# Relu-squared attention: score banks freed by the relu, gate units on one ring bank, the output factor a slot later, output projection behind the last gate unit

## The chip, the cores and the metric

One core of a Trainium2 chip runs the whole kernel in one launch. The metric is the device time of the execution in microseconds. The engines of the core work side by side, each on its own queue of instructions, and meet by semaphores: TensorE (PE, with its weight loads PEld) does matrix products and transposes into PSUM, VectorE (DVE) and ScalarE (ACT) read PSUM and SBUF, GpSimd (POOL) works on SBUF and issues the indirect DMAs, SyncE (SP) issues the plain DMAs.

## The reference, cut to what matters

Four blocks follow each other on 16 sequences of 256 tokens with 128 channels: a linear-recurrence attention, a mixture of 32 experts, a relu-squared attention, and a transformer block with 8 experts. The change touches the third alone:

```python
qg = split_heads(tokens @ Wqg, 16); kv = split_heads(tokens @ Wkv, 16)
queries, gates = qg[..., :16], qg[..., 16:]
keys, values = kv[..., :16], kv[..., 16:]
queries, keys, values = l2norm(queries), l2norm(keys), l2norm(values)
attn = square(relu(einsum('bhid,bhjd->bhij', queries, keys)))
aggr = einsum('bhij,bhjd->bhid', attn, values)
out = tanh(norm(aggr)) * aggr / norm(aggr) * tanh(silu(gates))
x = x + out.reshape(b, n, 1024) @ Wout
```

## The kernel before, in words

The kernel runs stage after stage, with all engines meeting between them. In the attention stage `pipeline` (line 76) carries the 16 sequences through five places, one place a step: `fetch` (gather the expert rows, combine them, normalise), `front` (project queries, keys, values and gates), `att` (scores, relu, square, aggregate), `tail` (norm of the aggregate, its factor, gating) and `end` (last gating, output projection, x3). A step thus works on up to five sequences. Fetch runs in steps 0 to 15, front in 1 to 16, att in 2 to 17, tail in 3 to 18, end in 4 to 19.

Each engine's queue is written out by hand in its own `half`, as eight slots g = 0 to 7, one for each pair of heads. The order in the source is the order on the engine; nothing is planned or reordered. An engine that waits for a semaphore holds everything behind it.

Scores of pair g go to two of the four score banks of PSUM (`scores`, line 1147), by turns. ScalarE's `relu` (line 858) reads both banks and writes a tile of SBUF, one of a ring of four. Five of the eight tiles are squared on VectorE (`square`, line 1679), which before the change multiplies the score banks by the relu's result; two on ScalarE (line 865), one on POOL (line 613). So before the change TensorE may overwrite score banks only when both relu and VectorE's square are done. `aggregate` (line 1163) multiplies the squares with the values; `take_aggregate` (line 883) copies two pairs' worth and frees those banks.

All other products of TensorE share two ring banks, 0 and 1. `fill` (line 1139) waits for the readers of the bank's last content. The tables `G_BANK`, `FT_BANK` and `F_BANK` (line 344) say which bank a gate unit (`project_gate`), a turned factor (`turn_factor`) and a spread factor (`spread_factor`) take. A gate unit goes through `unit_tanh` on ScalarE and `silu_unit` on VectorE (line 1702), which frees its bank.

The tail's chain is: `sum_squares` on TensorE, `norm_of` on VectorE (line 1688), `length_of` on POOL (o_inv, line 632), `tanh_of_norm` on ScalarE, `split_factor` on POOL (lines 639 to 649), `turn_factor`, `take_factor` on ScalarE (line 901), `spread_factor`, `gate_unit` on VectorE (line 1696), `output_of` on POOL (line 656).

The front's query and key chain ends on VectorE: `v_sum` (line 1747), `inverse_root` (from line 1661), the scaling of queries and keys (line 1800), the copy of the high part on ScalarE (line 940), `split_terms` (lines 1754 to 1758). Then TensorE's `turn_terms` (line 1223) transposes the terms. POOL scales the values (line 680) behind `length_of(tail, 1)`. VectorE's `combine` (line 1715) mixes the gathered rows: eight instructions of line 1722 with three inputs, then statistics. x3 is formed on line 1807.

## Time and profile before

| | us |
|---|---|
| median of 3 runs | 1832.07 |
| the three runs | 1829.85, 1848.20, 1832.07 |
| the profiled execution | 1849.76 |
| its span | 1848.1 |
| TensorE busy | 1281.9 (69%) |
| VectorE busy | 1097.8 (59%) |
| POOL busy | 902.4 (49%) |
| ScalarE busy | 755.9 (41%) |
| mean granted TensorE clock | 0.769 |

The span is the time between the first and the last instruction of the profiled execution. The granted clock is a share of TensorE's full speed (2.4 GHz); it stands at either full or half, so 0.81 means that 62% of a stretch ran at full. Busy shares are averages over stages with different limits; the attention stage lies between about 370 and 1171 us. A step of the pipeline is told by ScalarE's copy of x3T (line 958), which ends it: for instance at 604.4, 651.9, 791.7, 836.9 and 880.6 us.

### The profile page before, as it was taken

The numbers are of one execution on the slowest core, as the hardware profiler recorded it, in microseconds if no ns is written. First come the engines' busy times: TensorE is split into PE (matmuls) and PEld (weight loads), VectorE is DVE, ScalarE is ACT, GpSimd is POOL, SyncE is SP. The second block draws the span as 40 slices with busy tenths as digits, with TensorE's granted clock in tenths as the row PEclk, the third lists the DMA queues.
The fourth block names the chain that finished last, engine by engine and source line by source line (L and its number), as shares of the span: only waits on it lengthen the run. The fifth ranks groups of instructions, "written<-read, shape, count | busy, mean of one in ns | idle before, by whom it ended". The sixth has DMA issues, their size and how long they took to land. (4 is left out here: it accounts for less than half of the span.)

```text
span 1848.1 us, 26758 instructions
## 1 busy us (share of the span) xinstructions
PE 1281.9 (69%) x8186; PEld 770.1 (42%) x8187; DVE 1097.8 (59%) x2712; ACT 755.9 (41%) x1238; POOL 902.4 (49%) x1119
## 2 busy tenths in 40 slices
PE   3434331636788888888788888348888887847796
PEld 1222221413455555545455555324443443426685
DVE  7777771156666666666666653157787777743232
ACT  1101100315555555555555554026666665632221
POOL 2355567543566666666566644512332332225554
PEclk7555555667788888789788777559999988978766
DMA  4000001700000000000000000120000000001110
GB/s 135 22 15 26 14 2 37 143 16 5 2 8 8 7 7 8 7 7 7 8 7 7 4 4 4 43 72 10 18 11 18 18 18 10 13 19 46 40 42 11
DMA packets 73600, 41.61 MB, mean 23 GB/s; under 512 B 23979, under 2 KB 68908, under 8 KB 73476
## 3 DMA queue, kind: packets, MB, share of 16 engines
q1 hardware_dynamic: 50674, 24.02, 4.8%
q0 software_dynamic: 20432, 11.70, 3.1%
q10 hardware_dynamic: 2370, 4.35, 0.8%
q8 instruction: 65, 1.06, 0.3%
q14 instruction: 59, 0.48, 0.1%
HBM read 31.16 MB, written 23.87 MB: 30 GB/s over the span
## 5 line engine op out<-in xcount | busy, mean ns | idle before, releaser
L1864 DVE TENSOR_REDUCE terms<-psum 128x4 bf16<-128x1024 f32 x128 | 156.9, 1226 | 47.4 <-PE psum L1356 36.9
L1173 PE MATMUL psum<-attn,v 128*64 128x256 f32 x1024 | 163.9, 448 | 1.6 <-ACT aggT L886 1.6
L862 ACT ACTIVATE attn<-psum 128x1024 f32<-128x1024 f32 x128 | 130.5, 1019 | 81.7 <-PE psum L1160 81.5
L632 POOL TENSOR_TENSOR o_inv<-o_norm,minus_half 128x16 f32<-128x16 f32 x32 | 93.3, 2917 | 136.6 <-DVE o_norm L1688 136.6
L975 ACT ACTIVATE prob<-psum 128x512 f32<-128x512 f32 x256 | 138.7, 596 | 38.4 <-PE psum L1320 37.8
L623 POOL DMA_INDIRECT yg<-ye_dram,routel x128 | 131.6, 1028 | 45.1 <-issue 39.0
L714 POOL TENSOR_SCALAR veps<-meanvar 128x2 f32<-128x2 f32 x32 | 6.2, 193 | 294.5 <-DVE meanvar L1842 293.5
L576 POOL DMA_INDIRECT xe_dram<-rows_out,route x128 | 130.4, 1019 | 39.7 <-issue 39.1
L1333 PE MATMUL psum<-prob,v 128*32 128x256 f32 x1024 | 144.6, 406 | 0.7 <-ACT pvT L980 0.4
L1189 PE MATMUL psum<-x3T,w_g 128*128 128x256 f32 x256 | 77.7, 431 | 35.0 <-DVE silu_g L1702 20.1
L1683 DVE TENSOR_TENSOR attn<-psum,attn 128x1024 f32<-128x1024 f32 x80 | 97.0, 1212 | 6.1 <-ACT attn L862 3.1
L1173 PEld LDWEIGHTS psum<-attn,v 128*64 128x64 f32 x1024 | 69.6, 153 | 70.3 <-issue 35.6
L1253 PE MATMUL psum<-w_out,oT 128*128 128x128 f32 x512 | 87.0, 349 | 3.5 <-POOL oT L656 3.5
L1253 PEld LDWEIGHTS psum<-w_out,oT 128*128 128x128 f32 x512 | 84.0, 261 | 8.3 <-issue 8.3
L876 ACT ACTIVATE tanh_g<-psum 128x512 f32<-128x512 f32 x64 | 38.0, 593 | 114.1 <-PE psum L1189 114.1
L1198 PEld LDWEIGHTS psum<-pair_sum,agg_sq 128*128 128x128 f32 x512 | 77.1, 235 | 9.6 <-DVE kT L1713 6.9
L1160 PE MATMUL psum<-qT,kT 64*128 64x256 f16 x512 | 56.9, 305 | 33.1 <-DVE attn L1683 29.0
L1198 PE MATMUL psum<-pair_sum,agg_sq 128*128 128x2 f32 x512 | 77.2, 281 | 2.8 <-DVE kT L1713 1.9
L1356 PE MATMUL psum<-k_highT,q_highT 32*128 32x256 bf16 x512 | 53.9, 291 | 36.4 <-DVE terms L1864 35.5
L656 POOL TENSOR_TENSOR oT<-gate,aggT 128x1024 f32<-128x1024 f32 x32 | 75.5, 2358 | 5.6 <-remote 4.3
L1189 PEld LDWEIGHTS psum<-x3T,w_g 128*128 128x128 f32 x256 | 48.5, 205 | 68.4 <-issue 34.6
L1223 PE MATMUL psum<-ident,terms 128*128 128x128 f16 x512 | 54.1, 280 | 31.9 <-DVEq L1760 31.2
(308 smaller groups left out, 3050.7 us busy)
## 6 DMA issues: line engine op xcount, KB each, us to landing
x4n_dram<-x4n SPq DMA_DIRECT2D x16, 256.0 KB
w<-in_w POOLq DMA_DIRECT2D x48, 64.0 KB, 2.6
x_in<-in_x SPq DMA_DIRECT2D x8, 256.0 KB, 2.7
xe_dram<-zero_rows SPq DMA_DIRECT2D x8, 256.0 KB, 3.0
x_dram<-x1s SPq DMA_DIRECT2D x8, 256.0 KB
xe_dram<-rows_out,route POOLq DMA_INDIRECT x128
xe<-xe_dram SPq DMA_DIRECT2D x16, 128.0 KB
ye_dram<-ye SPq DMA_DIRECT2D x16, 128.0 KB, 2.2
```

Source lines behind the costliest of these rows:

```text
L576: pool.indirect_dma_start(xe_dram, bass.IndirectOffsetOnAxis(ap=where[:, j, K0 + k:K0 + k + 1], axis=0), rows_out[p][:, j, :], None, bound ...
L623: pool.indirect_dma_start(yg[fetch.p][:, j, k, :], None, ye_dram, bass.IndirectOffsetOnAxis(ap=where[:, j, K0 + k:K0 + k + 1], axis=0), bo ...
L632: n = chain.step(pool.tensor_tensor(o_inv[:], o_norm[:], minus_half[:].rearrange("q (j h) -> q j h", j=2), ALU.pow))
L862: act.activation(r[:], psum[:, 2 * (g % 2):2 * (g % 2) + 2, :], ACT.Relu).then_inc(s["relu_made"], 1)
L975: act.activation(prob[head % 4][:], bank[head % 3][:], ACT.Exp, scale=SCALE).then_inc(s["exp_made"], 1)
L1173: mm = pe.matmul(bank[4 + g % 4 // 2][DV * h:DV * h + DV, g % 2 * SEQ:(g % 2 + 1) * SEQ], v[q.p][:, c, head * DV:(head + 1) * DV], attn[g ...
L1189: mm = pe.matmul(b[:, c * SEQ:(c + 1) * SEQ], w_g[:, (2 * u + c) * P:(2 * u + c + 1) * P], x3T[:], start=True, stop=True)
L1198: mm = pe.matmul(b[:, HALF * j + 2 * c:HALF * j + 2 * c + 2], agg_sq[:, c, j * P:(j + 1) * P], pair_sum[:], start=True, stop=True)
L1253: mm = pe.matmul(b[:, j * D:(j + 1) * D], oT[:, c, j * P:(j + 1) * P], w_out[:, c, :], start=(c == 0), stop=(c == PAIRS - 1))
L1333: mm = pe.matmul(bank[3][part, t * SEQ:(t + 1) * SEQ], v4[q.q][:, c, head, :], prob[head % 4][:, c * SEQ:(c + 1) * SEQ], start=(c == 0), s ...
L1683: dve.tensor_tensor(r[:], psum[:, 2 * (g % 2):2 * (g % 2) + 2, :], r[:], ALU.mult).then_inc(s["attn_made"], 1)
L1864: dve.tensor_reduce(heads[:, :, jp, :], psum[:, 4:6, :].rearrange("q a (b k) -> q a b k", b=2), AX, ALU.max, negate=True).then_inc(s["max_ ...
```

## The change

Four things change, all in the attention stage.

1. VectorE's `square` multiplies the relu's tile in SBUF by itself. `scores` no longer waits for VectorE's squares, only for the relu two slots before.
2. All four gate units take ring bank 1 (`G_BANK`); the value blocks alternate between the banks (`V_BANK`), both turned factors take bank 0, the factor's spread and the sums of squares take banks by `F_BANK` and `NSQ_BANK`. Gate units 2 and 3 are projected ahead of an aggregation, in slots 4 and 5.
3. The factor of the tail's first half is turned in slot 2 and spread in slots 4 and 5; ScalarE copies it in slot 3. The second half is split on POOL in slot 5.
4. The output projection goes to slot 5, behind the last gate unit, and x3 behind the last silu.

With them VectorE's queue changes its order: the inverse root ahead of the second silu, then in slot 4 square, silu, gate unit and only then the combine; in slot 5 square, split of the terms, last silu, x3, gate unit. On ScalarE the high part is copied in slot 4 ahead of the gate's tanh, the squares of the last value blocks stand ahead of the square of the aggregate, and the query copy ahead of it.

```diff
--- before.py
+++ after.py
@@ -341,9 +341,11 @@
             s[name] = sem(name)
         N_SET = 14 + AHEAD
         ring = [bank[6], bank[7]]
-        G_BANK = (0, 0, 1, 1)
-        FT_BANK = (1, 0)
-        F_BANK = ((1, 0), (0, 0))
+        G_BANK = (1, 1, 1, 1)
+        V_BANK = (1, 0, 1, 0)
+        FT_BANK = (0, 0)
+        F_BANK = ((0, 1), (0, 0))
+        NSQ_BANK = (1, 0)
         SQUARED_BY = ("dve", "act", "pool", "dve", "dve", "act", "dve", "dve")
         SQUARE_DONE = {"dve": "attn_made", "act": "attn_made_act", "pool": "attn_made_pool"}
 
@@ -683,8 +685,9 @@
                         n = chain.step(pool.tensor_scalar(veps3[:], meanvar3[:, :, 1], 1.0, LN_EPS, ALU.mult, ALU.add))
                         chain.need(n)
                         pool.tensor_tensor(rstd3[:], veps3[:], minus_half[:, 0:2], ALU.pow).then_inc(s["rstd3"], 1)
+                    if tail and g == 5:
+                        split_factor(tail, 1)
                     if tail and g == 6:
-                        split_factor(tail, 1)
                         output_of(tail, 0)
                 chain.restart()
 
@@ -921,33 +924,34 @@
                             square_of(front, 2 + h, v[front.p][:, 0, 512 * h:512 * h + 512])
                     if tail and g == 1:
                         take_aggregate(tail, 1)
-                    if tail and g == 2:
-                        take_factor(tail, 0)
-                        square_aggregate(tail, 1)
                     if front and g == 2:
                         for h in range(2):
                             act.wait_ge(s["v_copied"], 4 * (front.n - 1) + h + 3)
                             square_of(front, 4 + h, v[front.p][:, 1, 512 * h:512 * h + 512])
+                    if tail and g == 2:
+                        square_aggregate(tail, 1)
+                    if tail and g == 3:
+                        take_factor(tail, 0)
                     if front and g == 3:
                         unit_tanh(front, 0)
                         unit_tanh(front, 1)
                     if front and g == 4:
-                        gate_tanh(front, 0)
                         unit_tanh(front, 2)
-                    if front and g == 5:
                         wait(act, s["terms_ps"], 4 * (front.n - 1))
                         act.wait_ge(s["qk_scaled"], front.n)
                         act.activation(terms[:, :, :, 0, :].rearrange("q j h d -> q (j h) d"), qk[:].rearrange("q j h d -> q (j h) d"), ACT.Copy).then_inc(s["high_made"], 1)
+                        gate_tanh(front, 0)
+                    if front and g == 5:
+                        unit_tanh(front, 3)
+                    if att and g == 5:
+                        take_aggregate(att, 0)
                     if tail and g == 5:
                         tanh_of_norm(tail, 1)
-                    if att and g == 5:
-                        take_aggregate(att, 0)
-                    if front and g == 5:
-                        unit_tanh(front, 3)
+                    if front and g == 6:
+                        take_q(front, 0)
                     if att and g == 6:
                         square_aggregate(att, 0)
                     if front and g == 6:
-                        take_q(front, 0)
                         gate_tanh(front, 1)
                     if tail and g == 7:
                         take_factor(tail, 1)
@@ -1146,11 +1150,7 @@
 
             def scores(att, g):
 
-                before_it = PAIRS * (att.n - 1) + g - 1
-                wait(pe, s["relu_made"], before_it)
-                if SQUARED_BY[g - 2] == "dve":
-                    by = SQUARED_BY.count("dve")
-                    wait(pe, s["attn_made"], by * (att.n - 1) + SQUARED_BY[:g - 1].count("dve") if g >= 2 else by * (att.n - 2) + SQUARED_BY[:g + PAIRS - 1].count("dve"))
+                wait(pe, s["relu_made"], PAIRS * (att.n - 1) + g - 1)
                 if g == 0:
                     pe.wait_ge(s["qkT_act"], 2 * att.n)
                     pe.wait_ge(s["qkT_dve"], 2 * att.n)
@@ -1192,7 +1192,7 @@
             def sum_squares(q, hf):
 
                 m = 2 * (q.n - 1) + hf + 1
-                b = fill(1, [(s["o_norm_made"], m)], [(s["aggr_sq_made"], m)])
+                b = fill(NSQ_BANK[hf], [(s["o_norm_made"], m)], [(s["aggr_sq_made"], m)])
                 for j in range(2):
                     for c in range(4):
                         mm = pe.matmul(b[:, HALF * j + 2 * c:HALF * j + 2 * c + 2], agg_sq[:, c, j * P:(j + 1) * P], pair_sum[:], start=True, stop=True)
@@ -1236,24 +1236,16 @@
                 elif tail:
                     readers[1] = [(s["o_norm_made"], 2 * (tail.n - 1) + 1)]
                 else:
-                    readers[1] = [(s["o_norm_made"], 2 * end.n)] if end else []
+                    readers[1] = [(s["gated"], 4 * (end.n - 1) + 2)] if end else []
                 for g in range(PAIRS):
                     if att:
                         scores(att, g)
                     if front and g == 0:
                         project_qk(front, 0)
                     if front and g == 2:
-                        project_v(front, 2, 0)
-                    if tail and g == 3:
-                        spread_factor(tail, 0, 0)
-                    if end and g == 4:
-                        b = fill(0, [(s["x3_made"], end.n)], [(s["o_made"], 2 * end.n)])
-                        for j in range(2):
-                            for c in range(PAIRS):
-                                mm = pe.matmul(b[:, j * D:(j + 1) * D], oT[:, c, j * P:(j + 1) * P], w_out[:, c, :], start=(c == 0), stop=(c == PAIRS - 1))
-                        mm.then_inc(s["y3_ps"], 1)
-                    if tail and g == 5:
-                        spread_factor(tail, 0, 1)
+                        project_v(front, 2, V_BANK[2])
+                    if front and g in (4, 5):
+                        project_gate(front, g - 2)
                     if front and g == 6:
                         turn_terms(front, 0, 0)
                     if att and g == 7:
@@ -1267,16 +1259,27 @@
                     if end and g == 0:
                         spread_factor(end, 1, 1)
                     if front and g == 1:
-                        project_v(front, 0, 1)
-                        project_v(front, 1, 0)
-                    if tail and g == 1:
+                        project_v(front, 0, V_BANK[0])
+                        project_v(front, 1, V_BANK[1])
+                    if front and g == 2:
+                        project_v(front, 3, V_BANK[3])
+                        project_gate(front, 0)
+                    if tail and g == 2:
                         turn_factor(tail, 0)
-                    if front and g == 2:
-                        project_v(front, 3, 1)
-                    if front and 2 <= g <= 5:
-                        project_gate(front, g - 2)
+                    if front and g == 3:
+                        project_gate(front, 1)
                     if tail and g == 3:
                         sum_squares(tail, 1)
+                    if tail and g == 4:
+                        spread_factor(tail, 0, 0)
+                    if end and g == 5:
+                        b = fill(0, [(s["x3_made"], end.n)], [(s["o_made"], 2 * end.n)])
+                        for j in range(2):
+                            for c in range(PAIRS):
+                                mm = pe.matmul(b[:, j * D:(j + 1) * D], oT[:, c, j * P:(j + 1) * P], w_out[:, c, :], start=(c == 0), stop=(c == PAIRS - 1))
+                        mm.then_inc(s["y3_ps"], 1)
+                    if tail and g == 5:
+                        spread_factor(tail, 0, 1)
                     if front and g == 6:
                         turn_terms(front, 0, 1)
                     if tail and g == 6:
@@ -1680,12 +1683,12 @@
 
                 dve.wait_ge(s["relu_made"], PAIRS * (q.n - 1) + g + 1)
                 r = attn[g % RING]
-                dve.tensor_tensor(r[:], psum[:, 2 * (g % 2):2 * (g % 2) + 2, :], r[:], ALU.mult).then_inc(s["attn_made"], 1)
+                dve.tensor_tensor(r[:], r[:], r[:], ALU.mult).then_inc(s["attn_made"], 1)
 
             def norm_of(q, hf):
                 wait(dve, s["o_len_made"], 2 * (q.n - 1) + hf)
                 dve.wait_ge(s["nsq_ps"], 2 * (q.n - 1) + hf + 1)
-                dve.tensor_scalar(o_norm[:], ring[1][:, 0:2 * HALF].rearrange("q (j h) -> q j h", j=2), 1e-24, None, ALU.max).then_inc(s["o_norm_made"], 1)
+                dve.tensor_scalar(o_norm[:], ring[NSQ_BANK[hf]][:, 0:2 * HALF].rearrange("q (j h) -> q j h", j=2), 1e-24, None, ALU.max).then_inc(s["o_norm_made"], 1)
 
             def gate_unit(q, hf, u):
 
@@ -1771,47 +1774,43 @@
                     if end and g == 0:
                         gate_unit(end, 1, 1)
                         kept = chain.step(dve.tensor_copy(x2_kept[:], x2[end.q][:]))
-                    if fetch and g == 4:
-                        combine(fetch)
                     if g > 0 and att and SQUARED_BY[g - 1] == "dve":
                         square(att, g - 1)
-                    if front and g == 1:
-                        take_v(front, 0, 1)
-                        qk_sum(front, 0)
-                        take_v(front, 1, 0)
-                        qk_sum(front, 1)
-                    if front and g == 2:
-                        take_v(front, 2, 0)
-                        v_sum(front, 0)
-                        take_v(front, 3, 1)
-                        v_sum(front, 1)
+                    if front and g in (1, 2):
+                        for k in (2 * g - 2, 2 * g - 1):
+                            take_v(front, k, V_BANK[k])
+                            if g == 1:
+                                qk_sum(front, k)
+                            else:
+                                v_sum(front, k - 2)
                     if front and g == 3:
                         silu_unit(front, 0)
-                    if tail and g == 3:
-                        gate_unit(tail, 0, 0)
-                    if front and g == 3:
                         v_sum(front, 2)
                         v_sum(front, 3)
-                        silu_unit(front, 1)
                         dve.wait_ge(s["sq_reduced"], 6 * front.n)
                         inverse_root(inv3[:], norm3[:], 6 * HEADS, s["inv_made"])
+                        silu_unit(front, 1)
                         qk3 = qk[:].rearrange("q j h d -> q (j h) d")
                         dve.wait_ge(s["inv_made"], front.n)
                         dve.tensor_tensor(qk3, qk3, inv3[:, 0:4 * HEADS].unsqueeze(2).to_broadcast([P, 4 * HEADS, DK]), ALU.mult).then_inc(s["qk_scaled"], 1)
                     if tail and g == 3:
                         norm_of(tail, 1)
-                    if end and g == 4:
+                    if front and g == 4:
+                        silu_unit(front, 2)
+                    if tail and g == 4:
+                        gate_unit(tail, 0, 0)
+                    if fetch and g == 4:
+                        combine(fetch)
+                    if front and g == 5:
+                        split_terms(front)
+                        silu_unit(front, 3)
+                    if end and g == 5:
                         wait(dve, s["x3_stored"][end.p], 16 * (end.k - 1))
                         dve.wait_ge(s["y3_ps"], end.n)
                         chain.need(kept)
                         dve.tensor_tensor(x3[end.p][:], x2_kept[:], ring[0][:, 0:2 * D].rearrange("q (j d) -> q j d", j=2), ALU.add).then_inc(s["x3_made"], 1)
-                    if front and g == 4:
-                        silu_unit(front, 2)
                     if tail and g == 5:
                         gate_unit(tail, 0, 1)
-                    if front and g == 5:
-                        split_terms(front)
-                        silu_unit(front, 3)
                     if front and g == 6:
                         take_k(front, 0)
                     if fetch and g == 6:
```

## Rows read from the trace of the kernel before

**Rows 1.** The page's first part: busy time of TensorE, share, instructions.
```profile
PE 1281.9 (69%) x8186; PEld 770.1 (42%) x8187; DVE 1097.8 (59%) x2712; ACT 755.9 (41%) x1238; POOL 902.4 (49%) x1119
```

**Rows 2.** Stretches: the attention stage, then two steps of it.
```profile
core 0: us, PE busy (x) PEld busy (x) DVE busy (x) ACT busy (x) POOL busy (x), PEclk, DMA share, GB/s
...
370.00:1171.00 801.00, 636.01 (x3712) 380.35 (x3712) 496.34 (x991) 405.34 (x544) 459.50 (x447) 0.81 0.03 7
...
604.40:651.90 47.50, 40.19 (x236) 24.89 (x234) 30.59 (x63) 25.38 (x34) 29.35 (x29) 0.81 0.03 7
...
836.90:880.60 43.70, 36.07 (x234) 21.69 (x233) 30.61 (x63) 25.10 (x34) 28.56 (x29) 0.91 0.03 8
```

**Rows 3.** TensorE's waits, 559.7 to 1071.7 (eleven steps): in total, times, longest.
```profile
PE psum L1223 <- DVEq L1760: 23.9, 11, 2.9
PE psum L1206 <- POOL factor L649: 18.0, 11, 1.7
PE psum L1160 <- DVE attn L1683: 13.8, 8, 3.0
```

**Rows 4.** Timeline, slots 1 and 2: start, duration, engine, line, work.
```profile
797.92 1.02 PE L1183 MATMUL psum<-w_v,x3T 128*128 128x512 f32 x2
...
800.57 1.01 ACT L886 ACTIVATE aggT<-psum 128x1024 f32<-128x1024 f32 x1
...
802.20 1.08 PE L1173 MATMUL psum<-attn,v 128*64 128x256 f32 x8
```

**Rows 5.** Timeline, slots 2 and 3: ScalarE up to the first silu.
```profile
802.64 1.04 ACT L891 ACTIVATE agg_sq<-aggT 128x1024 f32<-128x1024 f32 x1
...
805.18 0.63 ACT L870 ACTIVATE squares<-v 128x512 f32<-128x512 f32 x1 [0.98 <-DVE v L1709]
...
805.72 1.00 ACT L862 ACTIVATE attn<-psum 128x1024 f32<-128x1024 f32 x1
...
806.62 0.59 ACT L876 ACTIVATE tanh_g<-psum 128x512 f32<-128x512 f32 x1
...
807.31 0.69 DVE L1702 SCALAR_TENSOR_TENSOR silu_g<-tanh_g,psum 128x512 f32<-128x512 f32 x1 [1.65 <-ACT tanh_g L876]
```

**Rows 6.** Timeline, slots 3 to 6: VectorE, output projection, first terms.
```profile
808.52 1.27 DVE L1747 TENSOR_REDUCE norm<-squares 128x8 f32<-128x512 f32 x2
...
810.53 0.20 DVE L1661 TENSOR_SCALAR norm<-norm 128x96 f32<-128x96 f32 x1
...
811.78 3.18 PE L1253 MATMUL psum<-w_out,oT 128*128 128x128 f32 x27
...
814.13 1.22 DVE L1800 TENSOR_TENSOR qk<-qk,inv 128x1024 f32<-128x1024 f32 x1
...
816.03 1.92 DVE L1722 SCALAR_TENSOR_TENSOR x<-yg,routel,x 128x128 f32<-128x128 f32 x6
...
818.66 1.19 DVE L1683 TENSOR_TENSOR attn<-psum,attn 128x1024 f32<-128x1024 f32 x1
...
819.77 0.41 DVE L1807 TENSOR_TENSOR x<-x_kept,psum 128x256 f32<-128x256 f32 x1
...
821.83 0.68 DVE L1696 TENSOR_TENSOR gate<-gate,psum 128x512 f32<-128x512 f32 x1
...
823.44 1.23 DVE L1754 TENSOR_TENSOR terms<-qk,terms 128x1024 f16<-128x1024 f32 x1 [0.93 <-ACT terms L940]
...
825.73 1.01 PE L1223 MATMUL psum<-ident,terms 128*128 128x128 f16 x8 [1.70 <-DVEq L1760]
```

**Rows 7.** Timeline of step 1, where VectorE and POOL meet.
```profile
405.99 1.22 DVE L1800 TENSOR_TENSOR qk<-qk,inv 128x1024 f32<-128x1024 f32 x1
406.24 4.45 POOL L680 TENSOR_TENSOR v<-v,inv 128x2048 f32<-128x2048 f32 x1 [11.66 <-DVE inv L1672]
407.13 3.97 DVE L1722 SCALAR_TENSOR_TENSOR x<-yg,routel,x1l 128x128 f32<-128x128 f32 x2
```

**Rows 8.** Timeline, slot 4: POOL in the step of rows 4 to 6.
```profile
815.63 2.94 POOL L632 TENSOR_TENSOR o_inv<-o_norm,minus_half 128x16 f32<-128x16 f32 x1 [3.16 <-DVE o_norm L1688]
...
818.92 3.62 POOL L680 TENSOR_TENSOR v<-v,inv 128x2048 f32<-128x2048 f32 x1
```

## The prediction

> **What bounds the kernel now.** I read first the page's busy shares, then the stretches of the attention stage, then TensorE's waits, and last the timeline of one step. TensorE is the busiest engine, 69% of the span [rows 1]. The changed stage runs from about 370 to 1171 us; each step turns a new batch in, and a step that ends at 880.6 took 43.7 us at a granted clock of 0.91, one that ends at 651.9 took 47.5 us at 0.81 [rows 2]. The mean over 559.7 to 1071.7 is 512.0/11 = 46.5 us. Over those eleven steps TensorE waits 23.9 us for the query and key terms, 18.0 us for the output factor, 13.8 us for a VectorE square before it may overwrite score banks [rows 3]. That invites the thought that these 5 us a step are what the change removes. But a wait only pays if nothing else is late right behind it, so I follow one step (791.7 to 836.9 us) engine by engine.
>
> From the first silu unit, at 807.31 [rows 5], to the first transpose of the terms, at 825.73 [rows 6], 18.4 us pass. I took the same distance in the other steps, at fast and slow clock, and it hardly moves (18.4 to 18.8). VectorE fills it almost without a gap. So a step is three pieces: a head set by TensorE, ScalarE and the value copies, this middle set by VectorE, and a tail set by TensorE.
>
> **The head: the factor a slot later.** The wait for the factor stood after the values (797.92, two matmuls of 1.02 in all, end 798.94) and before slot 2. Moved, TensorE goes straight on: scores 0.33, third value matmul 1.02. Then the first aggregation needs the banks that ScalarE's copy of the last aggregate frees at 800.57 + 1.01 = 801.58 [rows 4]. That copy sits behind squares of the first two value blocks and does not move. The aggregation starts about 801.7 instead of 802.20: of 1.64 us [rows 3] some 0.5 is gained, the rest becomes a wait for the aggregate. Value blocks on alternate banks cost and gain nothing, since each copy is done by then.
>
> Behind it ScalarE has a new order. Before: relu, factor copy, agg_sq (802.64), two value squares, relu (805.72), tanh, silu at 807.31. After: both value squares (the second about 0.5 us earlier, 804.7, with its value block), agg_sq 1.04, relu 0.9, factor copy 0.26, tanh 0.69, silu. From 805.3, the end of that square, that is 1.0 + 0.9 + 0.26 + 0.69: silu at 808.1 [rows 5]. **Head: +0.75 us.** If ScalarE's handoffs hide more than I think the bound is 0; if the second square is no earlier, +1.3.
>
> **The middle, without contention.** Each row's duration less the 0.08 us by which successive VectorE rows overlap: silu 0.61, two sums 1.26, inverse root 3.60 (810.53 to 814.13), second silu 0.61, scaling and norm 1.23, square 1.11, third silu 0.60, gate 0.60, combine 3.30 (with scaling and norm, 814.13 to 818.66 less the 1.22), square 1.13, split 2.32, fourth silu 0.61, x3 0.41: 17.4 us [rows 5, 6]. TensorE's term transpose now needs x3 read out of its bank, and puts a factor spread and scores in front, after the fourth silu: 17.8 us against 18.4, **-0.6 us**. It is that little because the removed waits only let TensorE run ahead of VectorE. The gate units on one bank make a chain of matmul, tanh, silu, but VectorE's own order spaces the silus wider than the links of about 2.6 us, and the second unit's silu stands behind the inverse root, so the third unit waits some 2.3 us ahead of an aggregation. The output projection (3.18 us for 27 of its 32 matmuls [rows 6], so 3.8) goes under the combine; were it uncovered it would cost that. The split no longer waits for ScalarE (the 0.93 us in its row).
>
> **The squares from SBUF.** As an instruction it costs nothing: 1.19 us from PSUM, 1.22 us for the scaling, which reads two SBUF tensors of the same size [rows 6]. What changes is whom it meets. At 405.99 the scaling runs; POOL's scaling of v starts at 406.24 and takes 4.45 us, against 3.62 at 818.92. And the combine's first pair, at 407.13, takes 3.97 us where the later pairs take 0.64: it stands until v is done [rows 7, 8]; the 0.64 is a third of the 1.92 for six [rows 6]. So VectorE work with two SBUF inputs and this POOL work exclude each other. In the steady steps they miss each other now: v starts at 818.92, after the combine, and meets only work with one operand in PSUM, the squares among it.
>
> After the change the norm is ready at the same 815.5 (relative to the step; +0.0 with the head's delay against the saved silu), but POOL's o_inv (2.94) meets the square at once and starts 0.95 us late; v starts about 820.2. The combine now ends its two-input work at about 820.3, square 4 would start at 821.1, the split's subtraction behind it. v holds until 820.3 + 3.6 = 823.9. Square 4, or the end of the combine, waits 2.9 us, and split, fourth silu, x3 and the terms with it. Bounds: 0 (no exclusion for a square of a tile with itself, and a luckier order) and 3.6 (v's whole length); the nearest rows show 3.3 us lost by the pair at 407.13, so I take 2.9. **Middle: -0.6 + 2.9 = +2.3 us.**
>
> The Trainium skill (SBUF — State Buffer, section "SBUF: two separate sides") says that a VectorE instruction with two SBUF inputs and a GpSimd instruction that reads SBUF lock each other out for the whole instruction, whoever starts first. The two starts of [rows 7] agree. But the combine's six at 816.03 ran in 1.92 us under o_inv [rows 6, 8], which by the rule would have held them 2.5 us. By the rule the moved combine, due at 817.7, would also wait 1.75 us for the late o_inv, which ends about 819.5; that is 23 us more over 13 steps. I go by the rows.
>
> **The tail** has the same TensorE order. POOL's second factor split is free by then. SP's store waits for x3, and its next loads stand behind; x3 comes about 8 us later in the step, and the loads are wanted only in the next one, over 10 us later, so nothing. TensorE's clock is open. It idles about 5 us in front of the tail rather than 1.7; a slow tail costs up to 4 us (the two steps of [rows 2]), and no idle at all would save about as much. I take +0.5 us a step, bounds -2 and +2.
>
> **Sum.** Steps in which a fetch, front, attention and tail batch all exist: the fetch runs in steps 0 to 15, the tail from 3, so 13. 13 x (0.75 + 2.3) = 40; 13 x 0.5 = 6; ramps 0, as the two first steps already have the collision [rows 7]. +46 us. Against the profiled execution, 1849.8, this is 1896; that execution is 17.7 above the median of the runs, 1832.07, so I set the difference on the median: **1878 us**. About 1% (18 us) either way can't be told from no change.
>
> **Rivals.** (a) *Only the lock is wrong*: a square of a tile with itself takes no second port and the combine ends before v. Then 13 x (0.75 - 0.6 + 0.5) = +8, 1840 us. For it: no row has such a square beside POOL work. Against: the combine and the split have two inputs anyhow. Chance 0.17. (b) *Faster*: no lock, the head's ScalarE order hidden, TensorE's idle pieces shorter and the clock high in every tail: 13 x (-0.6 - 2.0) = -34, 1798 us. It decides where TensorE's idle time in the middle no longer brings the slow clock; for it, 5 us a step of waits do go. Chance 0.10. (c) *The lock by the whole instruction*, o_inv included: 13 x 1.75 more = 23, 1901 us. For it the row at 406.24; against, the combine under o_inv. (The Trainium skill's rule above.) Chance 0.10. The forecast: 0.63.
>
> Range: from 1826 (a, with the clock a little kind) to 1908 (c, with a slower tail). Slower by over 1%: 0.73 (forecast and c); within 1%: 0.17 (a and the ends of others); faster: 0.10.
>
> **What would show it.** Right: VectorE squares or combine instructions of over 3 us, next to POOL's v scaling; POOL's o_inv near 3.9 us; the first terms some 20.7 us after the first silu; the wait for the factor replaced by one for the aggregate; no TensorE wait for a VectorE square. Wrong: squares all at 1.22 us and v still at 3.62; then the step is a matter of the head and the clock. If the first silu is not later relative to the copy of x3T, the head was wrong.

## The result: 3.1% slower

| | us |
|---|---|
| after, median of 4 runs | 1895.71 (1894.91 to 1896.31) |
| before, median of 4 runs | 1836.72 (1829.85 to 1848.20) |
| ratio | 1.031, 95% interval 1.0263 to 1.0358 |
| profiled execution after, its span | 1895.82, 1894.1 |
| predicted | 1878 (1826 to 1908) |

The page's first part after the change, to hold against [rows 1]: every engine's busy time but TensorE's weight loads is up.

```profile
PE 1294.6 (68%) x8186; PEld 760.9 (40%) x8187; DVE 1143.9 (60%) x2712; ACT 757.4 (40%) x1238; POOL 923.1 (49%) x1119
```

VectorE has 2712 instructions as before and 46 us more in them. They are not more work: the eight instructions of the combine take 6.14 us a step where they took 2.81 (means of 13 steps), which is 43 of the 46. The rows below show them held up by POOL. A VectorE instruction that is held up in this way counts as busy, so the growth is a wait in disguise.

The stretches after (columns as in [rows 2]): ten steps, then the one that is followed below.

```profile
557.30:1072.70 515.40, 406.38 (x2342) 234.37 (x2343) 337.31 (x621) 253.60 (x341) 303.28 (x281) 0.80 0.03 7
813.20:864.50 51.30, 40.46 (x236) 23.22 (x238) 33.53 (x63) 25.34 (x35) 30.21 (x29) 0.81 0.03 6
```

A step takes 51.5 us instead of 46.5, at a granted clock of 0.80. With the copy of x3T as the mark, the 13 full steps run from 454.8 to 1123.4, 668.6 us; before they took 603.9 (467.8 to 1071.7). That is +64.7. The two ramp steps ahead of them are 3.6 shorter. This execution also spent 9.4 us less ahead of the first copy and 5.7 less behind the last one (the steps that empty the pipeline, and the rest of the program) than the profiled execution of before, which at 1849.8 lies above each of the four timed runs: 64.7 - 3.6 - 9.4 - 5.7 = 46.0, the difference of the two spans. That this is the very figure forecast is chance: the medians stand 59 apart.

TensorE's waits after, in the ten steps from 557 to 1072 (in total, times, longest), and POOL's largest:

```profile
PE psum L1213 <- DVE silu_g L1705: 53.6, 10, 5.4
PE psum L1189 <- DVE silu_g L1705: 33.1, 18, 2.5
PE psum L1173 <- ACT aggT L889: 13.8, 10, 1.4
POOL o_inv L634 <- DVE o_norm L1691: 70.4, 20, 4.2
```

All three waits of [rows 3] are gone, and the three largest are now others, 100.5 us in ten steps where there were 55.7 in eleven. The largest is once more a wait for VectorE: TensorE stands 5.4 us a step before it may write bank 1, for the last silu.

The head of the step that begins at 813.22 (start, duration, engine, line, work), to hold against [rows 4, 5]:

```profile
813.22 0.38 ACT L962 ACTIVATE x3T<-psum 128x256 f32<-128x256 f32 x1 [1.37 <-PE psum L1295]
813.75 2.05 PE L1179 MATMUL psum<-w_qk,x3T 128*128 128x512 f32 x2
819.61 1.98 PE L1183 MATMUL psum<-w_v,x3T 128*128 128x512 f32 x4
824.36 1.08 PE L1173 MATMUL psum<-attn,v 128*64 128x256 f32 x8 [1.39 <-ACT aggT L889]
830.67 0.69 DVE L1705 SCALAR_TENSOR_TENSOR silu_g<-tanh_g,psum 128x512 f32<-128x512 f32 x1 [2.85 <-ACT tanh_g L879]
```

Its middle, to hold against [rows 6, 8]:

```profile
836.43 1.22 DVE L1795 TENSOR_TENSOR qk<-qk,inv 128x1024 f32<-128x1024 f32 x1
837.65 1.22 DVE L1686 TENSOR_TENSOR attn<-attn 128x1024 f32<-128x1024 f32 x1
837.92 3.75 POOL L634 TENSOR_TENSOR o_inv<-o_norm,minus_half 128x16 f32<-128x16 f32 x1 [2.81 <-DVE o_norm L1691]
839.38 0.69 DVE L1705 SCALAR_TENSOR_TENSOR silu_g<-tanh_g,psum 128x512 f32<-128x512 f32 x1 [0.52 <-ACT tanh_g L879]
840.76 0.69 DVE L1699 TENSOR_TENSOR gate<-gate,psum 128x512 f32<-128x512 f32 x1 [0.69 <-PE psum L1213]
842.01 5.34 DVE L1725 SCALAR_TENSOR_TENSOR x<-yg,routel,x 128x128 f32<-128x128 f32 x6
842.02 3.62 POOL L682 TENSOR_TENSOR v<-v,inv 128x2048 f32<-128x2048 f32 x1
842.98 3.84 PE L1279 MATMUL psum<-w_out,oT 128*128 128x128 f32 x32
851.52 0.69 DVE L1705 SCALAR_TENSOR_TENSOR silu_g<-tanh_g,psum 128x512 f32<-128x512 f32 x1 [0.23 <-DVE terms L1761]
852.26 0.60 PE L1213 MATMUL psum<-fT,expand 24*128 24x256 bf16 x2 [5.45 <-DVE silu_g L1705]
853.34 1.04 PE L1223 MATMUL psum<-ident,terms 128*128 128x128 f16 x8
```

The six combine instructions that took 1.92 us take 5.34, and POOL's v, in the same 3.62 us, lies wholly inside them. The output projection runs at 842.98 without waiting; behind it TensorE stands until VectorE comes out of the combine, the square, the split and the last silu.

The same kind of step, cut in three as in the prediction, in means over the last 12 of the 13 full steps of each profiled execution (head: copy of x3T to first silu; middle: to the first transposed terms; tail: to the next copy):

| | head | middle | tail | step |
|---|---|---|---|---|
| before | 16.41 | 18.58 | 11.63 | 46.62 |
| after | 17.49 | 22.83 | 11.14 | 51.46 |

The middle of before hardly moves from step to step. Its tail does, from 8.50 to 13.55 us, and its profiled execution is 13 us above the median, which is up to 1 us a step if all of it lies here. So a difference of less than 1 us in the tail, against the row of before, is not firm.

### The profile page after: what moved, and what is told of

Same layout as the page of the kernel before. It is cut to its first block and busy times, and to the rows that moved or that the text cites. A ratio compares the mean times of both kernels' runs of the same rounds, so it can differ in the third digit from the quotient of the medians.

```text
span 1894.1 us, 26712 instructions
## 1 busy us (share of the span) xinstructions
PE 1294.6 (68%) x8186; PEld 760.9 (40%) x8187; DVE 1143.9 (60%) x2712; ACT 757.4 (40%) x1238; POOL 923.1 (49%) x1119
## 5 line engine op out<-in xcount | busy, mean ns | idle before, releaser
L1173 PE MATMUL psum<-attn,v 128*64 128x256 f32 x1024 | 174.5, 472 | 21.2 <-ACT aggT L889 21.2
L634 POOL TENSOR_TENSOR o_inv<-o_norm,minus_half 128x16 f32<-128x16 f32 x32 | 105.4, 3294 | 124.0 <-DVE o_norm L1691 124.0
L1189 PE MATMUL psum<-x3T,w_g 128*128 128x256 f32 x256 | 90.6, 487 | 62.4 <-DVE silu_g L1705 62.4
L1686 DVE TENSOR_TENSOR attn<-attn 128x1024 f32<-128x1024 f32 x80 | 99.2, 1240 | 3.5 <-issue 2.8
L1189 PEld LDWEIGHTS psum<-x3T,w_g 128*128 128x128 f32 x256 | 55.0, 233 | 94.9 <-DVE silu_g L1705 76.8
L1213 PE MATMUL psum<-fT,expand 24*128 24x256 bf16 x128 | 31.3, 334 | 81.3 <-DVE silu_g L1705 75.4
L1716 DVE COPY kT<-psum 128x1024 f16<-128x1024 f16 x32 | 22.1, 692 | 97.4 <-PE psum L1223 97.4
L1705 DVE SCALAR_TENSOR_TENSOR silu_g<-tanh_g,psum 128x512 f32<-128x512 f32 x64 | 43.9, 686 | 54.1 <-ACT tanh_g L879 50.6
L1336 PEld LDWEIGHTS psum<-prob,v 128*32 128x32 f32 x1024 | 49.8, 112 | 59.0 <-issue 28.5
L1183 PE MATMUL psum<-w_v,x3T 128*128 128x512 f32 x128 | 69.5, 650 | 1.2 <-DVE qk L1773 1.2
```

What stands on the lines that cost most here:

```text
L634: n = chain.step(pool.tensor_tensor(o_inv[:], o_norm[:], minus_half[:].rearrange("q (j h) -> q j h", j=2), ALU.pow))
L1173: mm = pe.matmul(bank[4 + g % 4 // 2][DV * h:DV * h + DV, g % 2 * SEQ:(g % 2 + 1) * SEQ], v[q.p][:, c, head * DV:(head + 1) * DV], attn[g ...
L1189: mm = pe.matmul(b[:, c * SEQ:(c + 1) * SEQ], w_g[:, (2 * u + c) * P:(2 * u + c + 1) * P], x3T[:], start=True, stop=True)
L1336: mm = pe.matmul(bank[3][part, t * SEQ:(t + 1) * SEQ], v4[q.q][:, c, head, :], prob[head % 4][:, c * SEQ:(c + 1) * SEQ], start=(c == 0), s ...
L1686: dve.tensor_tensor(r[:], r[:], r[:], ALU.mult).then_inc(s["attn_made"], 1)
```

## The experiments

The theory: VectorE work with two SBUF inputs and POOL's large tensor work exclude each other, and the change puts the combine on top of POOL's v. The first rival: it is the squares from SBUF. The second: it is the clock or the new order, with no lock ("lock" is short for this exclusion, and "v" for POOL's scaling of v). Each kernel's step, in the same cut; medians in us, head, middle and tail from its profiled execution:

| kernel | median | ratio to before (95%) | head | middle | tail |
|---|---|---|---|---|---|
| e1: after, squares from PSUM | 1883.17 | 1.0263 (1.0218 to 1.0307) | 17.56 | 22.47 | 11.03 |
| e2: after, combine first | 1833.79 | 0.9997 (0.9966 to 1.0027) | 17.56 | 20.20 | 9.07 |
| e3: both | 1817.81 | 0.9892 (0.9849 to 0.9935) | 17.35 | 19.96 | 9.11 |
| e4: before, squares from SBUF | 1862.61 | 1.0159 (1.0100 to 1.0218) | 16.74 | 20.05 | 10.58 |
| e5: after, POOL's v cut | 1838.48 | 1.0025 (0.9989 to 1.0061) | 17.13 | 19.08 | 11.33 |
| e7: before, combine behind a square | 1813.45 | 0.9856 (0.9780 to 0.9933) | 16.65 | 17.76 | 10.35 |
| e8: e3, ScalarE's old order | 1812.97 | 0.9885 (0.9820 to 0.9950) | 16.39 | 20.65 | 9.11 |
| e9: e8, combine last | 1796.32 | 0.9787 (0.9726 to 0.9849) | 17.14 | 18.21 | 9.09 |
| e10: before, output late | 1860.14 | 1.0126 (1.0063 to 1.0189) | 16.69 | 21.70 | 9.79 |
| e11: e7, output late | 1812.56 | 0.9887 (0.9854 to 0.9920) | 16.13 | 20.07 | 8.84 |
| e12: e3, output early | 1848.18 | 1.0047 (1.0015 to 1.0080) | 16.95 | 21.31 | 10.08 |
| e13: before, combine behind a silu | 1889.06 | 1.0290 (1.0228 to 1.0352) | 16.07 | 22.10 | 12.73 |

### e1: the squares read the score banks again

```diff
--- after
+++ e1
-                dve.tensor_tensor(r[:], r[:], r[:], ALU.mult)...
+                dve.tensor_tensor(r[:], psum[:, 2 * (g % 2):2 * (g % 2) + 2, :], r[:], ALU.mult)...
```

The wait of `scores` for the squares comes back with it.

> The changed kernel with one part undone: VectorE's squares read the score banks again and the scores wait for them. Theory (two-input work on VectorE and POOL's scaling of v exclude each other; the moved combine meets v): the six later instructions of the combine still take some 5.3 us against 1.9, o_inv is 2.9 again as the square before it has an operand in PSUM; the middle of a step (first silu to first terms) stays near 22.5 us; 1885 to 1898 us. Rival (the squares from SBUF carry the loss): the middle falls to about 19 us and the time to 1845.

The timeline of e1 in slot 4:

```profile
832.96 2.94 POOL L634 TENSOR_TENSOR o_inv<-o_norm,minus_half 128x16 f32<-128x16 f32 x1 [2.77 <-DVE o_norm L1695]
836.24 3.62 POOL L682 TENSOR_TENSOR v<-v,inv 128x2048 f32<-128x2048 f32 x1
836.38 3.89 DVE L1729 SCALAR_TENSOR_TENSOR x<-yg,routel,x1l 128x128 f32<-128x128 f32 x2
```

The square no longer delays o_inv, which is back at 2.94, and v starts earlier. It only means that v catches the combine's first pair instead of its third instruction: 3.89 us for the pair. The squares from SBUF are worth 0.36 us of middle here, and the middle stays at 22.47 where the rival asked for 19: the first rival is not the main cause. The time is 12.5 us below after and 2 us under the low end of what I expected.

### e2 and e3: the combine back ahead of the square

```diff
--- after
+++ e2
+                    if fetch and g == 4:
+                        combine(fetch)
                     if g > 0 and att and SQUARED_BY[g - 1] == "dve":
                         square(att, g - 1)
...
                     if tail and g == 4:
                         gate_unit(tail, 0, 0)
-                    if fetch and g == 4:
-                        combine(fetch)
```

e3 is e2 with the edit of e1.

> The changed kernel with the combine back in front of the square in slot 4; squares still from SBUF. Theory: the combine runs free under o_inv, and now a square stands for v, some 2.4 us in the place of 3.4; the middle about 21 us, 1870 to 1882 us, squares of over 3 us in the rows. Rival (only the combine's place counts, a square of a tile with itself locks nothing): all squares 1.22 us, the middle 19 us, about 1850 us.

> Both parts undone: squares from PSUM with the scores' wait, combine in front of the square; banks, gate units, factor and output projection as changed. Theory: nothing on VectorE waits for v, the middle about 19 us, the head still 0.75 us longer than before: 1845 to 1855 us, that is 40 to 50 us back. Rival (the gate units on one bank and the ScalarE order carry the loss): above 1875 us.

e2's timeline in slots 4 to 6:

```profile
804.21 1.92 DVE L1725 SCALAR_TENSOR_TENSOR x<-yg,routel,x 128x128 f32<-128x128 f32 x6
808.07 3.62 POOL L682 TENSOR_TENSOR v<-v,inv 128x2048 f32<-128x2048 f32 x1
809.14 3.62 DVE L1686 TENSOR_TENSOR attn<-attn 128x1024 f32<-128x1024 f32 x1
811.61 4.60 PE L1279 MATMUL psum<-w_out,oT 128*128 128x128 f32 x32
816.79 0.62 PE L1223 MATMUL psum<-ident,terms 128*128 128x128 f16 x8
```

One line moved up in VectorE's queue takes back the whole loss: 62 us less than after, more than twice what I had expected of it. e3 also came out 27 us under my range. The combine runs in 1.92 us and v locks a square instead, for 2.4 us over its 1.22. Yet e2's middle is only 0.24 us longer than e3's, where that square takes 1.22, because by now something else ends the middle. From e3, a square that runs beside v (801.20 to 804.82), then the output projection and x3:

```profile
803.24 1.22 DVE L1690 TENSOR_TENSOR attn<-psum,attn 128x1024 f32<-128x1024 f32 x1
805.96 4.31 PE L1283 MATMUL psum<-w_out,oT 128*128 128x128 f32 x32
810.36 0.42 DVE L1815 TENSOR_TENSOR x<-x_kept,psum 128x256 f32<-128x256 f32 x1 [2.68 <-PE psum L1283]
```

VectorE waits 2.68 us for the output projection: with the lock gone, the projection's late place ends the middle. What I had left out of both expectations is the second half of the gain. The tail is 2.1 us shorter than after (9.1 against 11.1). The projection now ends right at the terms, instead of leaving TensorE idle for 5.4 us. The stretches of the two tails, after and then e3:

```profile
853.30:864.50 11.20, 10.66 (x78) 6.89 (x78) 3.89 (x8) 6.21 (x8) 5.72 (x4) 0.68 0.10 24
```

```profile
810.80:820.00 9.20, 8.53 (x79) 5.78 (x78) 4.45 (x8) 6.00 (x7) 5.48 (x3) 0.85 0.13 31
```

The granted clock is 0.85 of full instead of 0.68 in these two, and the first eight transposes take 0.62 us (e2 above) instead of 1.04. e3 as a whole is 1.1% faster than before.

### e4: the squares from SBUF alone

```diff
--- before
+++ e4
-                dve.tensor_tensor(r[:], psum[:, 2 * (g % 2):2 * (g % 2) + 2, :], r[:], ALU.mult)...
+                dve.tensor_tensor(r[:], r[:], r[:], ALU.mult)...
```

`scores` waits for the relu alone, as in the changed kernel.

> The kernel before with one part done: squares from SBUF, scores wait for the relu alone. Theory: square 4 meets v and waits 2.2 to 2.8 us in each full step, so the middle goes from 18.5 to about 21 us and the time up by 25 to 36 us, to 1862 to 1873. Rival (the squares are harmless and freed banks help): TensorE's wait for the squares goes, 1815 to 1837 us.

Timeline and TensorE's longest wait of e4:

```profile
815.11 3.62 POOL L680 TENSOR_TENSOR v<-v,inv 128x2048 f32<-128x2048 f32 x1
815.92 3.89 DVE L1679 TENSOR_TENSOR attn<-attn 128x1024 f32<-128x1024 f32 x1
```

```profile
PE psum L1219 <- DVEq L1756: 46.5, 11, 4.4
```

A square takes 3.89 us beside v, and the wait for the terms goes from 23.9 us in eleven steps [rows 3] to 46.5. So the change's first part, squares from SBUF and score banks freed early, costs 1.6% by itself in the old order, where the split stands close behind the locked square.

### e5: POOL's v cut short

```diff
--- after
+++ e5
-... pool.tensor_tensor(vv, vv, inv3[:, 4 * HEADS:]...
+... pool.tensor_tensor(vv[:, 0:1, :], vv[:, 0:1, :], inv3[:, 4 * HEADS:4 * HEADS + 1]...
```

> The changed kernel with POOL's scaling of v cut to one head of 32 (the other values stay unnormalised): 0.3 us in the place of 3.6, so that there is nothing left to lock out. Theory (the lock itself costs, not the order of the queues): the combine's six run in 1.9 us again, the middle falls from 22.8 to 19.5-20.2 us and the time by 33 to 44 us, to 1850-1862. Rival (the combine is late and VectorE's order, gate units and banks cost by themselves): the middle stays above 21.5 us and the time above 1880.

The timeline of e5 in slot 4:

```profile
799.76 3.75 POOL L634 TENSOR_TENSOR o_inv<-o_norm,minus_half 128x16 f32<-128x16 f32 x1 [2.80 <-DVE o_norm L1691]
803.65 1.95 DVE L1725 SCALAR_TENSOR_TENSOR x<-yg,routel,x 128x128 f32<-128x128 f32 x6
803.85 0.30 POOL L682 TENSOR_TENSOR v<-v,inv 128x64 f32<-128x64 f32 x1
```

The kernel leaves out the scaling of all heads of the values but one, so its output is not the reference's; it serves as a measurement only. With everything else as in the changed kernel, a short v gives the combine its 1.95 us and the kernel its old time (1.031 becomes 1.0025). This is the nearest to a direct proof: nothing on VectorE, ScalarE or TensorE was touched, and the order of their queues is the same. The middle falls by 3.75 us, more than the 3.4 of the lock; the time is 12 us under the low end of what I expected. The tail stays at 11.33 in the mean (9.54 to 12.45), though the lock is gone and TensorE now waits only 2.1 us for the last silu.

### e7 and e13: how far back may the combine go?

```diff
--- before
+++ e7
-                    if fetch and g == 4:
-                        combine(fetch)
                     if g > 0 and att and SQUARED_BY[g - 1] == "dve":
                         square(att, g - 1)
+                    if fetch and g == 4:
+                        combine(fetch)
```

e13 puts it two instructions further, behind x3 and `silu_unit(front, 2)`.

> The kernel before with one line moved: the combine behind the square in slot 4, squares from PSUM, all else as before. Theory: the combine now reaches into POOL's scaling of v and stands for it; the middle goes from 18.6 to about 22 us, the time up by 35 to 45 us, to 1870-1880. Rival (the order alone is harmless): TensorE's score wait of 1.3 to 3 us in slot 5 goes, 1820 to 1840 us.

> The kernel before with the combine two steps further back than in the seventh run: behind the square, x3 and the third silu of slot 4; squares from PSUM. In the seventh run the combine ended 0.1 us after POOL's scaling of v began and so went free. Theory (the lock decides, by who starts first): here v starts first, the combine's first instruction stands up to 3.6 us, the time goes 25 to 45 us above the seventh's 1813, to 1840-1860. Rival (on the kernel before a later combine is free): 1805-1820.

Timeline of e7 and a wait of its TensorE, then the timeline of e13 and its TensorE's largest wait:

```profile
800.20 1.92 DVE L1722 SCALAR_TENSOR_TENSOR x<-yg,routel,x 128x128 f32<-128x128 f32 x6
801.99 3.62 POOL L680 TENSOR_TENSOR v<-v,inv 128x2048 f32<-128x2048 f32 x1
```

```profile
PE psum L1213 <- DVE x L1807: 14.9, 9, 3.0
```

```profile
835.85 3.62 POOL L680 TENSOR_TENSOR v<-v,inv 128x2048 f32<-128x2048 f32 x1
836.34 0.69 DVE L1702 SCALAR_TENSOR_TENSOR silu_g<-tanh_g,psum 128x512 f32<-128x512 f32 x1 [2.30 <-ACT tanh_g L876]
836.95 2.93 DVE L1722 SCALAR_TENSOR_TENSOR x<-yg,routel,x1l 128x128 f32<-128x128 f32 x2
```

```profile
PE psum L1160 <- DVE attn L1683: 57.7, 10, 6.5
```

e7 came out 57 us under the low end of what I expected. I had it collide, but the combine's last instruction was already running when v came (it ends at 802.12, v starts at 801.99), and the next large instructions behind it have one operand in PSUM. What it gains is the place of the square, which now frees the score banks ahead of the combine. TensorE's 13.8 us of waits for a square [rows 3] are gone, but TensorE gets little of them: it stands 14.9 us for x3 instead. The scores come earlier, though, and with them ScalarE's copy of the high part: VectorE's split waited 9.5 us for that copy in eleven steps of before, and 0.5 in e7. That is the size of the 0.82 us by which the middle is shorter. The tail is 1.28 shorter in the mean; against before's tail that is not much more than is firm.

In e13, two instructions further back, the same combine's first pair stands 2.93 us instead of 0.60. That is 2.3 of the 4.3 us that the middle grows from e7 to e13. About as much is no lock: the third silu now stands ahead of the combine, and VectorE has nothing to do for 2.30 us until its tanh is there. In e7 the combine filled that time. Behind both, the square and with it the score banks are late, and the tail gets the slow clock (12.73 us, a granted clock of 0.54 from 846.5 to 859.8). I had put e13 at 1840 to 1860; it is 29 us above that, and I had counted the lock alone. From e7 to e13 are 76 us. The same line of code is worth -1.4% or +2.9%; whether it ends ahead of v decides about half of the difference in the middle.

### e8 and e9: the best version

```diff
--- e3
+++ e8
+                    if tail and g == 2:
+                        square_aggregate(tail, 1)
                     if front and g == 2:
                         for h in range(2):
...
-                    if tail and g == 2:
-                        square_aggregate(tail, 1)
```

```diff
--- e8
+++ e9
...
+                        silu_unit(front, 1)
                         dve.wait_ge(s["sq_reduced"], 6 * front.n)
                         inverse_root(inv3[:], norm3[:], 6 * HEADS, s["inv_made"])
-                        silu_unit(front, 1)
...
+                    if fetch and g == 5:
+                        combine(fetch)
                     if end and g == 5:
                         wait(dve, s["x3_stored"][end.p], 16 * (end.k - 1))
```

On POOL, v then comes ahead of `length_of(tail, 1)`, and `split_factor(tail, 1)` ahead of the deviation.

> The third experiment (squares from PSUM, combine first, the rest as changed) with one ScalarE order put back: the square of the aggregate ahead of the last two value squares in slot 2. Theory (the head got longer because ScalarE's relu and tanh stand behind a value square that waits for its copy): the head falls from 17.4 to about 16.4 us, the time by 8 to 14 us, to 1804-1810. Rival (the head is set by the wait for the aggregate's banks): no change, 1818 +-4.

> The eighth experiment with the combine behind the last silu, the second silu ahead of the inverse root again, and on POOL the scaling of v ahead of o_inv and the factor's split ahead of the deviation. Theory: v runs beside VectorE work with a PSUM operand, the combine beside o_inv and small work, and 3.3 us of combine go from in front of the square, silu and output projection; the middle about 18 us, the time 20 to 30 us below the eighth, 1778-1790. Rival (TensorE's own work sets the middle there): within 8 us of the eighth.

e8 shortens the head by 0.96 us as expected and gives 0.69 of it back in the middle, whose end is the output projection: the time is 5 us below e3's, 3 above my range, and the intervals of the two ratios overlap. e9's timeline in slots 3 to 6:

```profile
779.58 1.22 DVE L1799 TENSOR_TENSOR qk<-qk,inv 128x1024 f32<-128x1024 f32 x1
779.90 4.39 POOL L680 TENSOR_TENSOR v<-v,inv 128x2048 f32<-128x2048 f32 x1 [1.68 <-DVE inv L1679]
784.26 1.28 DVE L1761 TENSOR_TENSOR terms<-qk,terms 128x1024 f16<-128x1024 f32 x1
787.93 1.97 DVE L1729 SCALAR_TENSOR_TENSOR x<-yg,routel,x 128x128 f32<-128x128 f32 x6
```

Here v meets the scaling, which came first: it is v that stands 0.77 us over its 3.62, and POOL has the time. The split starts as v ends, and the combine fills the time under the output projection. 1796.32 us, 2.1% faster than before and 5.2% faster than after; I had expected 20 to 30 us below e8 and it was 17.

### e10, e11 and e12: the place of the output projection

```diff
--- before
+++ e10
-                    if end and g == 4:
+                    if end and g == 5:
                         b = fill(0, [(s["x3_made"], end.n)], [(s["o_made"], 2 * end.n)])
...
```

In e10 the projection follows the last gate unit in TensorE's slot 5, and x3 the last silu; e11 is the same on e7; e12 takes both back to slot 4 in e3.

> The kernel before with the output projection (and x3) alone moved to slot 5, behind the last gate unit. Theory A (a dense run of matmuls just ahead of the tail lets the tail run at full clock): the tail falls from 11.6 to 9-9.5 us, the middle grows by 1-1.5, 1815 to 1830 us. Theory B (the tail's gain in the third run came from gate units and banks): tail 11-12 us, 1835 to 1855 us.

> The kernel before with the combine behind the square of slot 4 (as in the seventh run) and the output projection late. Under theory A the two gains add in part: 1795 to 1810 us; under B 1812 to 1825 us.

> The third run (squares from PSUM, combine first, the rest as changed) with the output projection and x3 back in slot 4. Under theory A the tail goes back from 9.1 to 11-12 us and the time to 1825-1845 us; under B the tail stays and the middle gets shorter, 1805 to 1818 us.

The late projection shortens the tail each time (11.63 to 9.79, 10.35 to 8.84, 10.08 to 9.11). Whether that pays is the middle's affair. In e10 the middle grows by 3.1 us: the early projection ran in time in which TensorE would otherwise wait for the norm and a square, and with it gone that time is empty. TensorE's waits in e10:

```profile
PE psum L1189 <- DVE o_norm L1688: 26.4, 11, 3.3
PE psum L1160 <- DVE attn L1683: 26.0, 11, 2.4
```

e10 is some 20 us slower than before: my theory A had a gain, and its rival, 1835 to 1855, is missed as well. The tail did nearly what A said (9.79, where it had 9 to 9.5); what I had too small was the middle, 3.1 us where I had 1 to 1.5. e11 has the same time as e7 (1812.6 and 1813.5): 1.5 us won in the tail, 2.3 lost in the middle, 0.5 won in the head; I had expected 1795 to 1810 of A. With the new bank plan the late place is right: early costs 30 us (e12 against e3), 1.35 us a step in the middle and 0.97 in the tail. e12's tail went to 10.08, not to the 11 to 12 that I had expected.

## Why the prediction was right, point by point

**The pieces.** Forecast in the 13 full steps: +46; measured +64.7. On the medians it is +59 against +46. The forecast's sign, its mechanism and its range held; the head and the middle were right in kind. The size was helped by luck: the middle was 25 us too small over 13 steps and the head 4, and a tail 13 below the forecast and ramps of -3.6 made up for more than half of it.

**Head, +0.75 a step: right, in the order's part.** The wait for the factor became one for the aggregate (18.0 us in eleven steps [rows 3], 13.8 in ten now). Counted from the first value matmul, the aggregation comes 4.75 us behind (819.61 to 824.36) instead of 5.24 (796.96 to 802.20 before): 0.49 gained, for which I had written "some 0.5". From the same mark the first silu comes 11.06 us behind instead of 10.35: +0.71. The mean head rose by 1.08. The remaining 0.37 lies ahead of the first value matmul and is the clock: from the copy of x3T to that matmul pass 5.28 us where the first query and key matmuls took 1.10, and 6.3 to 6.8 where they took 2.05, but for one long step in each kernel (11.43 and 9.91). Of the last 12 steps 5 began slow in before and 9 after. e8 undoes the ScalarE order and shortens e3's head by 0.96, 0.80 of it behind the first value matmul.

**Middle, +2.3: right in kind, short by 1.95.** The followed step is 22.67 against 18.42. The lock took 3.4 us (5.34 less 1.92) where I took 2.9: I had v arrive at the end of the combine, and it arrived at its third instruction. (By my own rows v was due at 819.9, not 820.2: 815.63 + 0.95 and the 3.29 from the start of o_inv to that of v in [rows 8].) Two waits I had taken as covered were not: the third silu stands 0.52 us for its tanh, the gate unit 0.69 for the spread factor, both behind matmuls at the slow clock (the third gate unit 2.08 us for four matmuls, the second 1.13; the wait ahead of the third, which I had at 2.3, was 0.94). From the last x3 to the transpose went 0.8 us instead of 0.4, at the slow clock too. The inverse root was 0.35 shorter (832.58 to 835.83, where I took 3.60). Together 0.5 + 1.21 + 0.4 - 0.35 = 1.76 of the 1.95; the rest was not followed.

**Squares.** "As an instruction it costs nothing" held: 1.22 us alone. POOL's o_inv at 3.75 (forecast 3.9) fits the meeting with the square; in e1, where that square has an operand in PSUM, it is 2.94. That the square itself would be locked came true in e2 and e4, and in the last ramp of after, where POOL's oT is its partner:

```profile
1190.59 2.35 POOL L658 TENSOR_TENSOR oT<-gate,aggT 128x1024 f32<-128x1024 f32 x1 [2.36 <-remote]
1190.70 3.33 DVE L1686 TENSOR_TENSOR attn<-attn 128x1024 f32<-128x1024 f32 x1 [0.69 <-ACT attn L865]
```

So rival (a), in which such a square is not locked, is wrong. In the steady steps of after, though, the victim was the combine.

**Tail, +0.5: measured -0.49.** That is within the 1 us that before's tail leaves open, so whether the sign was wrong stays open too. I set a slow tail against before's as if before's were fast; most of them were not (11.63 in the mean), as these two stretches of before show:

```profile
825.70:836.90 11.20, 10.45 (x76) 6.80 (x78) 4.46 (x8) 5.35 (x8) 6.52 (x6) 0.72 0.01 1
779.50:791.70 12.20, 11.92 (x76) 8.23 (x78) 4.36 (x8) 5.21 (x8) 6.54 (x6) 0.58 0.01 1
```

What I did not see is that the late output projection could have shortened the tail by 2 us. It is not the lock itself that kept it from doing so: e5 has no lock and a tail of 11.33, while e2 keeps a locked square and has 9.07. What the two slow ones share is a combine behind the gate unit, so that VectorE is later than the projection and TensorE idles ahead of the tail (5.4 us in after, 2.1 in e5, none in e2). The bound of -2 that I set for the clock is what e2 and e3 have.

**Rival (b), faster,** was wrong for this kernel, and right for its neighbours: e3, two edits away, and e9 have no lock that VectorE stands in, hardly any idle time ahead of the tail, and most of the tail at the high clock (0.85 in the stretch of e3). That comes near its conditions. They run in 1818 and 1796 us; it said 1798. **Rival (c), the lock by the whole instruction, o_inv included,** comes near in time (1901), for another reason. By the Trainium skill (SBUF — State Buffer, section "SBUF: two separate sides") a VectorE instruction with two SBUF inputs and POOL work that reads SBUF exclude each other for the whole instruction. The runs agree for v, in both directions, and for oT, which held a square; they don't for o_inv on 128x16, under which e2's six combine instructions ran in 1.92 us (804.21, o_inv from 803.81 for 2.94), as in [rows 6, 8]. o_inv itself is held up when it comes second (3.75).

**Ramps, 0:** they gained 3.6 us. The collision of [rows 7] is not gone from them but has moved in both, from the combine to the scaling (4.46 us at 395.34, behind v at 395.11). In the same cut the first of them has 13.26, 16.28 and 5.28 us where before had 13.79, 17.13 and 6.04; the second has 11.60, 18.55 and 13.47 where before had 13.75, 21.78 and 9.62. So heads and middles are shorter by 6.8 and the tails longer by 3.1.

**Still open:** how much of the tail's gain in e3 is due to the dense projection ahead of it rather than to the shorter idle time. e5's tail stays at 11.33 with 2.1 us of idle, e7's is 10.35 with the projection early; the runs show where the clock was high, not what is enough for it. No run undoes the bank plan or the later factor alone; e5 says only that these and the new order together come to nothing against before (1.0025), and e3, e8 and e9 that other orders gain with the same banks.

## What to carry to other kernels

When an edit moves VectorE work with two SBUF operands, lay POOL's large tensor instructions beside it in the timeline first: in one queue of 46 us the same eight instructions cost 2.55 us or nearly 6. Look for idle time that the moved work used to fill as well; in e13 that was as dear as the lock. A VectorE instruction whose duration is its own plus what is left of a POOL instruction is a wait, though no view of waits lists it. And a removed wait pays only where something that ends a piece starts earlier by it. Freed score banks gained 0.8 us of middle in e7, where the split had waited behind them; in e4 they bought nothing that shows, and their price (there a second SBUF operand) was paid in full.

## What the runs showed of the hardware beyond that

- Both inputs from the same tile count as two: the square of a tile with itself took 3.33, 3.62 and 3.89 us beside POOL work, 1.22 alone; with one input in PSUM it took 1.22 beside the same POOL instruction (e3, 803.24).
- The exclusion works both ways: v takes 3.62 us when it comes first, and 4.39 when it starts 0.32 us behind the scaling (e9).
- A POOL `pow` on 16 columns, 2.94 us long, did not hold up the six combine instructions that ran beside it (1.92 us in e2), but took 0.8 us longer behind a square from SBUF (3.75 in after and e5).
- The block of 32 matmuls moved to right ahead of the tail shortened the tail in all three pairs that differ only in its place and that of x3 (11.63 to 9.79, 10.35 to 8.84, 10.08 to 9.11 us). In two single stretches the granted clock of the tail was 0.85 with the block right ahead (e3) and 0.68 with 5.4 us of idle time between (after).
